# TensorE products of 512 columns issued as two of 256, in a kernel of two time-mix layers and a routed mixture of experts

## The reference

```python
# h: 4 x 2048 tokens of 256 features
def time_mix(x, ln_w, ln_b, Wk, Wv, Wr, Wo):          # two layers of it
    n = layer_norm(x, ln_w, ln_b)
    k, v, r = n @ Wk.T, n @ Wv.T, sigmoid(n @ Wr.T)
    state[t] = 0.95 * state[t-1] + 0.05 * (k * v)[t]   # a scan along the tokens
    return x + (r * state) @ Wo.T
x = layernorm(h + time_mix(time_mix(h, ...), ...))
# experts: E = 8, each token goes to its best 2; hidden width 512
top_v, top_i = top_k(x @ Wg.T, 2);  probs = softmax(top_v)
y = sum over e of  w_e * ((silu(x @ W1[e].T) * (x @ W2[e].T)) @ W3[e].T)
out = layernorm(x + y)
```

## Time and profile before

| | |
|---|---|
| median of 3 runs | 1275.16 us (1272.74 to 1279.75) |
| the profiled execution | 1267.26 us, its span 1265.5 us |
| mean granted clock of PE | 0.953 |
| busy share of the span | PE 87%, PEld 78%, DVE 73%, ACT 52%, POOL 69% |
| products on PE | 7172, of them 2112 with 512 columns |

### The profile page before, as it was taken

How to read it: one execution, slowest core, us unless ns; L and a number is a source line. 1 busy time by engine, 2 the same in 40 slices (tenths; PEclk the granted TensorE clock), 3 DMA queues, 4 the chain that set the end, 5 groups by cost and what they waited for, 6 DMA issues and landing times. The chain is left out here.

```text
span 1265.5 us, 23767 instructions
## 1 busy us (share of the span) xinstructions
PE 1106.2 (87%) x7172; PEld 990.4 (78%) x7172; DVE 926.1 (73%) x1973; ACT 658.4 (52%) x1091; POOL 869.1 (69%) x696
## 2 busy tenths in 40 slices
PE   7899888888888988738999999999999999999910
PEld 6777777777677777636888888888899999999910
DVE  6687888878887888746766666666667888888737
ACT  4455455555555444425544554445555666666618
POOL 3455777777877777667567776667667777777634
PEclk9999999999999999959999999999999999999965
DMA  3011111111111010237556665566669898888659
GB/s 150 17 51 67 43 43 52 51 50 50 50 50 39 31 48 34 67 102 196 146 148 161 158 153 142 140 155 159 148 156 229 240 228 247 227 244 227 141 165 384
DMA packets 80662, 164.20 MB, mean 130 GB/s; under 512 B 27424, under 2 KB 45600, under 8 KB 80352
## 3 DMA queue, kind: packets, MB, share of 16 engines
q1 hardware_dynamic: 49248, 126.16, 31.6%
q0 software_dynamic: 31360, 37.38, 15.7%
HBM read 118.01 MB, written 45.49 MB: 129 GB/s over the span
## 5 line engine op out<-in xcount | busy, mean ns | idle before, releaser
L1163 POOL DMA_INDIRECT x_acc<-fy_sb,pair_out x142 | 285.5, 2011 | 149.0 <-DVE fy_sb L1264 80.2
L1319 PE MATMUL fring<-fxh,fw_hi 128*128 128x256 f32 (+1 forms) x816 | 264.9, 325 | 3.6 <-DVE fxl L1255 1.9
L1321 PE MATMUL fring<-fxh,fw_lo 128*128 128x256 f32 (+1 forms) x816 | 265.4, 325 | 0.0
L1320 PE MATMUL fring<-fxl,fw_hi 128*128 128x256 f32 (+1 forms) x816 | 264.9, 325 | 0.0
L1182 ACT ACTIVATE fw_hi<-w_raw 128x1024 fp32r<-128x1024 f32 x153 | 161.1, 1054 | 150.0 <-PE fy L1362 138.7
L1235 DVE TENSOR_TENSOR fw_lo<-w_raw,fw_hi 128x1024 fp32r<-128x1024 f32 x153 | 186.5, 1219 | 17.9 <-ACT fw_hi L1182 17.0
L88 POOL DMA_INDIRECT xg<-x_src,pair_in x142 | 159.0, 1120 | 43.3 <-issue 42.7
L78 POOL DMA_INDIRECT slot_list<-pairs,slot_u x128 | 148.3, 1159 | 47.3 <-issue 30.5
L1319 PEld LDWEIGHTS fring<-fxh,fw_hi 128*128 128x128 f32 x816 | 153.7, 188 | 17.2 <-issue 2.3
L1320 PEld LDWEIGHTS fring<-fxl,fw_hi 128*128 128x128 f32 x816 | 153.7, 188 | 13.4
L1321 PEld LDWEIGHTS fring<-fxh,fw_lo 128*128 128x128 f32 x816 | 153.8, 188 | 13.2
(11 more groups left out here) (148 smaller groups left out, 2330.0 us busy)
## 6 DMA issues: line engine op xcount, KB each, us to landing
w_raw<-w_ffn SPq DMA_DIRECT2D x153, 512.0 KB
x_in<-h SPq DMA_DIRECT2D x16, 512.0 KB, 3.3
x_src<-x SPq DMA_DIRECT2D x16, 512.0 KB
x_acc<-x SPq DMA_DIRECT2D x16, 512.0 KB
acc<-x_acc SPq DMA_DIRECT2D x16, 512.0 KB, 7.6
out<-o SPq DMA_DIRECT2D x16, 512.0 KB, 6.6
xg<-x_src,pair_in POOLq DMA_INDIRECT x142
x_acc<-fy_sb,pair_out POOLq DMA_INDIRECT x142
```

What stands on the lines that cost most here:

```text
L1163: nc.gpsimd.indirect_dma_start(x_acc, bass.IndirectOffsetOnAxis(pair_out[j][:, q, 0:1].bitcast(U32), 0), y[j][:, q, :], None, compute_op=A ...
L1319: nc.tensor.matmul(out, hi, rows_hi, start=dc == 0, stop=False)
L1320: nc.tensor.matmul(out, hi, rows_lo, start=False, stop=False)
L1321: last = nc.tensor.matmul(out, lo, rows_hi, start=False, stop=dc == DC - 1)
```

## The change

Each product of 512 moving columns is issued as two of 256 columns. In `project` a loop over the two parts of a bank stands outside the loop over `dc`: the six products of the left half come first, then the six of the right half. In `hidden`, the part loop that small blocks had already now runs twice for every block; with a large block it walks the left and the right half of the same 512 rows, with a small block the two pieces of the hidden width, as it did. Each half bank is an accumulation of its own (`start` and `stop` in each). The waits and the semaphore that tells of a full bank stay where they were. No other engine's program is touched.

```diff
+SPAN = CH // 2
 ...
                     out = bank(l, e, m, j)
                     col = m * D + e * P
-                    for dc in range(DC):
-                        hi, lo = w_hi[:, l, dc, col:col + P], w_lo[:, l, dc, col:col + P]
-                        nc.tensor.matmul(out, hi, xh[l][:, dc, :], start=dc == 0, stop=False)
-                        nc.tensor.matmul(out, hi, xl[l][:, dc, :], start=False, stop=False)
-                        last = nc.tensor.matmul(out, lo, xh[l][:, dc, :], start=False, stop=dc == DC - 1)
+                    for part in range(CH // SPAN):
+                        cols = slice(part * SPAN, (part + 1) * SPAN)
+                        for dc in range(DC):
+                            hi, lo = w_hi[:, l, dc, col:col + P], w_lo[:, l, dc, col:col + P]
+                            rows_hi, rows_lo = xh[l][:, dc, cols], xl[l][:, dc, cols]
+                            nc.tensor.matmul(out[:, cols], hi, rows_hi, start=dc == 0, stop=False)
+                            nc.tensor.matmul(out[:, cols], hi, rows_lo, start=False, stop=False)
+                            last = nc.tensor.matmul(out[:, cols], lo, rows_hi, start=False, stop=dc == DC - 1)
                     last.then_inc(s_pg[l], 1)
 ...
-                    for part in range(CH // n):
-                        hb = u * (CH // n) + part
-                        out = ring[2 * (u % 2) + i][:, part * n:(part + 1) * n]
+                    for part in range(CH // SPAN):
+                        hb, first = u * CH // n + part * SPAN // n, part * SPAN % n
+                        out = ring[2 * (u % 2) + i][:, part * SPAN:(part + 1) * SPAN]
                         for dc in range(DC):
                             col = PART[i][0] + dc * H + hb * P
                             hi, lo = w_hi[:, j, col:col + P], w_lo[:, j, col:col + P]
-                            rows_hi, rows_lo = xh[:, dc * n:(dc + 1) * n], xl[:, dc * n:(dc + 1) * n]
+                            cols = slice(dc * n + first, dc * n + first + SPAN)
+                            rows_hi, rows_lo = xh[:, cols], xl[:, cols]
```

## The result

The changed kernel takes 1287.91 us (median of 10 runs, 1283.35 to 1295.21); the kernel before 1276.09 us (median of 10, 1270.61 to 1282.92; three of them are those of the table ahead). The ratio is 1.0108, with the interval 1.008 to 1.0136. The kernel is slower by 11.8 us by the medians and by some 14 us by the ratio, where 6 had been forecast. The profiled execution of the changed kernel took 1287.46 us with a span of 1285.7 us.

A forecast was written before the change was run, and what follows sets the result against it. PE's distances between product starts were taken to bound the expert phase. Large blocks +5.8 us and attention +0.5 us made +6.3 us, on 1275.16 giving 1281.5, stated as 1281 us; range 1265 to 1289.

The forecast's parts named there:

- attention paying all: Rival, attention: PE late handing over banks, so +0.43 us a step stands on the cycle; +6.9 us, 1288 us, chance 0.12.
- code: Rival, attention loop: longer body not held, jumps back wait for code; +2.4 to +12 us, 1284 to 1293, chance 0.05.
- the first two, before 600 us, still wait for rows and weights at a mixed clock; 18 count: Start of the large blocks: only 18 of 20 blocks were costed, the first two left out of the sum.
- the large blocks, "+5.8 us": Large blocks: all 256-column products 117.9 ns apart, a block 17.84 us, +0.32 us each over 18 blocks, +5.8 us.
- With only 256s in the stream the interval holds from block to block, and changes only after a stop of PE: Read from small blocks: distance between products stays 113.3 or 117.9 ns; about 26 of 31 blocks have the longer.
- Attention, "+0.5 us": Attention: only six old products between `picked` and the output product lack cover; 6 ns each over 14 steps, +0.5 us.
- the cover of 2.4 us a step before `picked`: Attention: PE already waits 2.4 us a step for `picked`, covering the doubled products' +0.43 us a step.
- the sign named for it: Attention steps: PE's wait for `picked` would be shorter by about 0.4 us, with steps as long as before.
- the 3 us that the prediction named as a sign against it: End of attention: the prediction would be wrong if that end moved by more than 3 us.
- The end of a bank: From the last starts to ACT's and DVE's start: 1.57 us before, 1.58 us after, counted as nothing.
- The short interval: Rival, large blocks: 256-column products 113.3 ns apart, -5.6 us, perhaps -8.3 us in small blocks; 1261 to 1269.5, chance 0.17.
- the alternation stays: Rival, large blocks: successive runs take 118 and 113 ns in turns, 17.52 us a block stays; 1275 us, chance 0.11.

## Why the prediction was right or wrong

The sign held, and the measured time lies inside the range. The size failed: +6.3 us was forecast, +12 measured by the medians and +14 by the ratio. That 1287.91 us is still inside 1265 to 1289 is owed to the rivals' width (attention paying all, code), and neither of those rivals came true.

**The step that failed: "the first two, before 600 us, still wait for rows and weights at a mixed clock; 18 count".** The two blocks were costed at nothing, and most of the loss stands in them. Splitting them alone gives 1283.52 against 1275.61 us, +7.9; splitting the eighteen others alone gives no measurable difference. The price is no price of products. PE's completions come up to 11 us late beside or behind POOL's scatters to the list, and with the scatters gone the change costs 1.8 us, at most 6.7. From the first block's start to the third's the changed kernel takes 47.8 and 47.1 us, the kernel before 37.0 and, in the trace with the long wait, 46.8. In the earlier trace rows the stretch looked like part of a smooth stage, and one trace was taken for the kernel, while the unchanged kernel has executions with and without the long wait. Its place in the first trace, DVE waiting 5.07 us for something "remote" inside the second block, was there to be asked about.

**The term that was mis-sized: the large blocks, "+5.8 us".** Measured is 299.5 - 297.9 = 1.6 us over 17 blocks. The two intervals of 113 and 118 ns, and no third one, were right. "With only 256s in the stream the interval holds from block to block, and changes only after a stop of PE" failed at the eight transposes, and the stream of a large block is not one of 256s alone. It makes two long blocks in three. The average block rose by 0.1 us instead of 0.32.

**Attention, "+0.5 us", in two parts.** For the loop it was right: the steps are as long as before, as the cover of 2.4 us a step before `picked` said, though the sign named for it did not come (the wait fell by 0.5 us in six steps and not by 0.4 in each). At the ends it was too little. The last three distances between products for the ranks add up to 55.4 us in both traces of the changed kernel, and to 52.8 and 53.9 us in those of the kernel before, some 2 us that the six steps of the earlier trace rows could not show. The first large block starts at 575.5 and 574.0 us against 570.1 and 572.1, 3.6 us later on average, which is over the 3 us that the prediction named as a sign against it. All traces together make it less: six with attention split have their first block at 574.4 us on average, nine with attention whole at 572.3, 2.1 us apart, and the last three distances are 2.1 us apart as well. The rival that attention pays all of it (+6.9) is excluded: twelve steps at +0.43 us would make 5.2 us from the first to the thirteenth product for the ranks, and 0.4 was measured. That splitting attention alone gave +0.79% is in its trace half a later start (first block at 576.1 us, 6.0 us after the first trace's) and half the wait (43.2 us for the first two distances against 37.0, the second being 25.34).

**What held.** The end of a bank cost nothing: in the steady blocks a bank takes 1.58 us from its first start to its last end at the long interval, as computed. The code rival is false: 35 packets of code as computed, none between 242.8 and 462.0 us while the attention loop of 928 loads and products ran. DVE, ACT and POOL stayed off the bound in the steady expert phase. The short interval did not take hold. Of the rival "the alternation stays" something came true, for the intervals still take turns, but two to one.

The small blocks, which are not touched, take 214.9 and 216.0 us from the start of block 26 to that of the last against 213.4 and 214.2, within what they vary by (212.2 to 217.3 in all traces).

The account of +11.8 us: large blocks 1.6, attention's end about 2, and 8 for the late completions with the 1.2 GHz stretch behind them. The first term is read from traces that agree among themselves to 0.5 us (299.5 to 300.0 in five with these blocks split, 297.9 to 298.1 in seven with them whole). The last is +7.9 measured by splitting two blocks alone, of which 0.6 at most is intervals; by its ratio (1.0029 to 1.0088) it may be 4 to 11. The second is 2.1 us by all traces, with single traces 0.4 to 4.6 apart in the last three distances. That these terms meet 11.8 so closely is partly luck.

**Open.** Why PE's completions come late beside these scatters, and why splitting products in the first blocks, or at attention's end, makes common what the unchanged kernel has only in some executions (in how many is not known, as only two were traced). The trace has the semaphore events behind the products, and nothing that shows what holds them back. That two scatters a block still hurt the changed kernel says that it isn't their number alone.

## What to carry to other kernels

A product of 256 columns (113 ns) stands just above the distance under which no fp32r product of the large blocks with its own 128-column weight load came here (111 ns; the 32-bit transposes came at 99), so halving 512 was nearly free in the steady state and halving again took a block from 17.6 to 27.9 us; measure that least distance before choosing a width. Before costing a change from one trace, look whether the total's spread hides two kinds of executions, and ask of each short stretch at a phase's start what "remote" is; what 95% of the program does says nothing of the block where three engines meet for the first time. A change that is neutral in the steady state should be tried with its first and last pieces left alone: here that version (the split from the third large block on) costs nothing measurable.

## What the runs showed of the hardware

- Products of fp32r behind their own weight loads came 229 to 233 ns apart with 512 columns, 113 or 118 ns with 256, and 111 ns with 128 in every product of the large stage.
- The interval of 256s changes between its two values, 4% apart, at a group of transposes, in an order that came back in every trace of split large blocks (17.84, 17.64, 17.41 us in seven traces).
- Semaphore events of PE stood up to 11 us behind its products beside eight indirect scatters of pairs, with a lateness that grew from bank to bank. The long ones moved with the scatters, and without the scatters none over about 1 us was left in the first blocks. In four traces (the first one of the kernel before, attention alone, its loop alone, and the large blocks from the third on) they came behind the scatters, beside the gathers that POOL issues next.
- In the steady large blocks of the changed kernel the event of one of the two banks of `fy` stood mostly 1.3 to 2.2 us behind its last product, that of the other 0.01 us.
- Where PE stood for about 12 us, the granted clock fell to 0.5 before it began again, for 13.7 us in five traces and 17.1 in a sixth, and came back to 1.0 between 3.4 and 6.0 us after the new start; without the scatters it stayed at 1.0 from 579 us to the end of the large stage.
